# A delta-net decoder layer: beta on the scan's diagonal by ScalarE, both tables from PSUM by VectorE, the last two levels' evictions by ScalarE

## Chip, cores and metric

One core of a Trainium2 chip runs the whole program. The metric is the device time of one execution in microseconds; of several executions the median is given.

## What is computed

One pre-norm decoder layer on x of 8 x 256 tokens and 512 channels: x plus a gated delta net, plus cross attention, plus a feed-forward network. The change touches the delta net alone. Its recurrence per head, with normalised keys k, gates b (beta) and decays d, is

```
Sk    = einsum('bhi,bhipj->bhpj', k_t, state)
delta = (v_t - Sk) * b_t[..., None]
state = state * d_t + einsum('bhi,bhpj->bhipj', k_t, delta)
o     = einsum('bhi,bhipj->bhpj', q_t, state)
```

k, q and v come from a projection of the normalised x and a causal convolution with 4 taps. Behind the recurrence o is RMS-normed, multiplied by silu(z) and projected back. There are 16 key heads with 2 value heads each, and the recurrence runs over the 256 tokens of a batch element.

## The kernel before, in words

`delta_net` works in 64 sections: 16 key heads (`hk`) times 4 windows of 512 tokens (`bp`), each window two blocks of 256 tokens. A section treats NM = 4 matrices, one per block and value head. The recurrence is turned into matrix form. Two tables are made per matrix, in three 128 x 128 pieces each (TRI = 384 columns): `a_t`, keys against keys, times decay products and beta, and `b_t`, keys against queries, the same way. The decay products are a scan on VectorE (L779) over the decays, with an identity `diag` as its added operand, so that each row starts at 1 on the diagonal. The new values `delta` solve a triangular system with `a_t`: its two 128 x 128 diagonal chunks c = 0, 1 are inverted by doubling in LEVELS - 1 = 6 levels, and `b_t` then gives the output.

Each engine has its own program (`pe_section`, `act_section`, `dve_section`, the GpSimd loop), and the order of its instructions is written out by hand. Engines wait for each other by counted events, as `E["xm"]`: nothing on an engine passes a waiting instruction. While section s is inverted, the projections and convolutions of section s + 1 and the output of section s - 1 are woven into the gaps.

The order in a section:
- TensorE: transposes of v (L437), norms of the outputs of s - 1 (L445), half of the key projection (L405), start of the inverse (`pe_first`, L473). Then for each level: `pe_x` (L483, writes `xp`), half a projection of s + 1 or an output product of s - 1 (`pe_y`, L460, at levels 4 and 5), and `pe_tu` (L493, L496; L500 at level 6), which needs `x_l`, the masked copy of `xp` in SBUF. Between 5 and 6 stands one more output product. Then the solution with L506, the gate projections as fill, the products keys x keys and keys x queries of s + 1 (`pe_kq`, L425), and the output product (L576).
- VectorE: at the head of a section the a table from SBUF copies (L789, eight operations, with beta as a scalar), 1 - a (L794), the first inverse matrices (L801), gating of s - 1 (L809, L814), and per level the masked copy `x_l` (L852) and one convolution (L756, three taps). Output sums (L819) stand around levels 4 to 6. Behind the levels come the differences L827, L834, L871, the rounding L873 and the four scans.
- ScalarE: evictions of PSUM, among them `act_kq` (L714), the levels' evictions (L680), the convolution inputs (L609, L612), exponentials and logarithms, and the rounding of the right side (`v_r`, L692) at level 4.
- GpSimd: the b table from SBUF copies in 16 operations (`pool_b`, L975 to L981), the remainders of the gated outputs (L985), silu (L990), and the split of weights in two parts (L965, L967).

The eight PSUM banks are `pj0`, `pj1`, `xp0`, `xp1`, `tp`, `up`, `ms0` and `ms1`; `ms` and `up` hold the `pe_kq` products and `ms` also the norms.

Of the kernel before, what the change touches and what calls it, by code (L numbers as in the profile page):

```python
# [278 lines left out]
def delta_net(nc, y_all, xh, xl, w_d, conv_w, cols, lmask, half_mask, diag, beta, decay_rows):  # L279
# [10 lines left out]
    with ExitStack() as ctx:  # L290
        m = Memory(nc, ctx)
        NM = 2 * PV
        WC = KT * P
# [15 lines left out]
        kk = m.sb("kk_masked", [P, 2, TRI])  # L309
        qk = m.sb("qk_masked", [P, 2, TRI])  # L310
# [5 lines left out]
        kk16, ez16 = kk[:, :, :].rearrange("p b t -> p (b t)").bitcast(F16), [e[:, :].bitcast(F16) for e in ez]  # L316
        W = NM * P
        H = W // 2
        pair = [kk16[:, 0:2 * W], ez16[1][:, 0:2 * W]]
# [17 lines left out]
        tu_bank = (tp, ms[1])  # L337

        E = {}
        for name, n in dict(  # L340

                pj=4, cin=4, c3=4, cv=12, pz=2, ez=2, zc=2, e1=2, lz=2, rz=2, sz=2,
                beta_s=1, conv_t=1,

                ksq=1, kssp=1, kss=1, kln=1, krn=1, kn=1, kq=4, km=4, dec=4,

                vt=2, vc=2, vr=1, at=8, bq=8, bt0=4, bt=4, an=2, u0=2, t0=2,

                xp=2 * LEVELS - 2, xm=2 * LEVELS - 2, tu=2 * LEVELS - 2, tc=2 * LEVELS - 2, uc=2,

                d0p=2, d0=2, rd0=2, rp=2, res=2, dp2=2, delta=2, cp=1, rhs1=1, rhs1r=1,

                op=2, osq=2, oss=2, oln=2, ors=2, g1=2, g2=2, ghi=2, glo=2, y=4, yadd=4).items():
            E[name] = m.event("e_" + name, n)
# [56 lines left out]
        def pe_norms(pe, t):  # L411

            E["ksq"].wait(pe, t, 0)
            pe.matmul(ms[0][:, :], ones, ksq[:, :], start=True, stop=True).then_inc(E["kssp"].sem, 1)
# [25 lines left out]
        def pe_out_norms(pe, s, p, more):  # L440

            E["osq"].wait(pe, s, p)
            if more:
                E["km"].wait(pe, s + 1, 3)
            pe.matmul(ms[p][:, :], ones, osq[p][:, :], start=True, stop=True).then_inc(E["oss"].sem, 1)  # L445
# [19 lines left out]
        def pe_first(pe, s, c, after_out):  # L465

            E["u0"].wait(pe, s, c)
            if c == 0 and after_out:
                E["delta"].wait(pe, s + -1, 1)
            elif after_out:  # L470
                E["oln"].wait(pe, s + -1, 1)
# [15 lines left out]
        def pe_tu(pe, s, lv, c):  # L487

            E["xm"].wait(pe, s, 2 * (lv - 1) + c)
# [20 lines left out]
        def pe_section(pe, s, bp, hk, prev, nxt):  # L510
# [133 lines left out]
        def act_out_norms(act, s, p):  # L644
            E["oss"].wait(act, s, p)
            act.activation(gat[p][:, :], ms[p][:, :], ACT.Ln, scale=1.0 / P, bias=cols["rms_eps"])\
# [13 lines left out]
        def act_section(act, s, bp, hk, prev, nxt):  # L660
# [15 lines left out]
            for lv in range(1, LEVELS):  # L676
                for c in range(2):
# [27 lines left out]
            if nxt:  # L705
                act_kq(act, s + 1, 0)
                act_kq(act, s + 1, 1)
                act_kq(act, s + 1, 2)
                act_kq(act, s + 1, 3)
            act_sigmoid(act, s, 1)  # L710

        def act_kq(act, t, i):
            E["kq"].wait(act, t, i)
            act.activation((kk, qk)[i % 2][:, i // 2, :], (ms[0], ms[1], up, ms[0])[i][:, 0:TRI], ACT.Copy)\  # L714
                .then_inc(E["km"].sem, 1)

        def act_prologue(act):
            first = Section(0, 0)
            for j in range(GATE):
# [3 lines left out]
            for i in range(4):  # L723
                act_kq(act, first, i)
# [9 lines left out]
        def dve_beta(dve, s, bp, hk):  # L734

            E["bt"].wait_before(dve, s)
# [37 lines left out]
        def dve_decays(dve, t, q):  # L774

            if q == 0:
                rows_in.wait(dve, t, 31)
            i = slot(q)
            dve.tensor_tensor_scan(dec[:, i, :], dec[:, i, :], diag, 0.0, ALU.mult, ALU.add).then_inc(E["dec"].sem, 1)  # L779

        def dve_a(dve, s):

            E["km"].wait(dve, s, 3)
            E["beta_s"].wait(dve, s, 0)
            for q in range(NM):
                E["dec"].wait(dve, s, q)
                for c, sl in enumerate((slice(0, SEQ), slice(SEQ, TRI))):
                    before = dec[:, slot(q), sl.start + c:sl.stop + c]
                    dve.scalar_tensor_tensor(out=a_t[:, q, sl], in0=kk[:, q // PV, sl],  # L789
                                             scalar=beta_s[:, 2 * (q // PV) + c, q % PV:q % PV + 1], in1=before,  # L790
                                             op0=ALU.mult, op1=ALU.mult).then_inc(E["at"].sem, 1)
            E["at"].wait(dve, s, 7)
# [43 lines left out]
        def dve_section(dve, s, bp, hk, prev, nxt):  # L836
            t, nhk, nbp = s + 1, (nxt or (0, 0))[0], (nxt or (0, 0))[1]
            dve_beta(dve, s, bp, hk)
            dve_a(dve, s)
            if prev:  # L840
                dve_gated(dve, s + -1)
            if nxt:
                dve_conv_weights(dve, t, nhk)
            for lv in range(1, LEVELS):
                if lv in (5, 6) and prev:
                    dve_y(dve, s + -1, prev[1], 2 * lv - 9)
                for c in range(2):
# [5 lines left out]
                       .then_inc(E["xm"].sem, 1)  # L853
                if lv == 4 and prev:
# [19 lines left out]
            dve_gate(dve, s, 0)  # L874
            if nxt:
                dve_decays(dve, t, 1)
            dve_rest(dve, s, 1)
            if nxt:
                dve_decays(dve, t, 2)
            dve_residual(dve, s, 1)  # L880
# [3 lines left out]
            E["dp2"].wait(dve, s, 1)  # L884
            dve.tensor_tensor(delta[1], tp[:, :], d0[:, :].bitcast(F32), ALU.add).then_inc(E["delta"].sem, 1)

        def dve_prologue(dve):
# [3 lines left out]
            dve_conv_weights(dve, first, 0)  # L891
            for j in range(GATE):
# [3 lines left out]
            for q in range(NM):  # L896
                dve_decays(dve, first, q)

        def dve_epilogue(dve, s, hk):
            dve_gated(dve, s)  # L900
            for i in range(4):
# [27 lines left out]
        def load_decays(sp, hk, bp):  # L929

            if hk or bp:
                E["at"].wait(sp, hk * NSEC + bp - 1, 7)
# [36 lines left out]
        def pool_b(pool, s, q):  # L969
            E["km"].wait(pool, s, q // PV * 2 + 1)  # L970
            E["beta_s"].wait(pool, s, 0)
            if s:
                E["op"].wait(pool, s - 1, PV - 1)
            for c, sl in enumerate((slice(0, SEQ), slice(SEQ, TRI))):
                pool.tensor_scalar(b_t[:, q, sl], qk[:, q // PV, sl], beta_s[:, 2 * (q // PV) + c, q % PV:q % PV + 1],  # L975
                                   None, ALU.mult).then_inc(E["bq"].sem, 1)
            E["dec"].wait(pool, s, q)
            E["bq"].wait(pool, s, 2 * q + 1)
# [1062 lines left out]
```

## Time and profile before

| | before |
|---|---|
| median of 3 executions | 4521.77 us (4520.63 to 4523.58) |
| the profiled execution | 4521.22 us |
| its span, first to last instruction | 4519.4 us |
| TensorE matmul busy | 3998.6 us (88%) |
| VectorE busy | 3161.6 us (70%) |
| ScalarE busy | 2237.8 us (50%) |
| GpSimd busy | 1898.3 us (42%) |

The profile is one execution: 4521.22 us is its whole time, 4519.4 us the span of its instructions, and the 1.8 us between lie around them. PE is TensorE's matmuls, PEld its weight loads, DVE VectorE, ACT ScalarE, POOL GpSimd. Busy shares are of the whole span; the delta net is about its first 3100 us. In an order in time, the number in brackets is how long the engine stood idle before the row, and behind it the instruction that released it. Matmuls overlap, so the step from one start to the next is the time that one costs.

### The profile page before, as it was taken

How to read it: one execution, taken by the hardware profiler on the slowest of the kernel's cores; microseconds unless marked ns; L12 is line 12 of the kernel's file. 1: busy time of each engine (PE TensorE's matmuls, PEld its weight loads, DVE VectorE, ACT ScalarE, POOL GpSimd, SP SyncE). 2: the span in 40 equal slices, each digit the busy share in tenths (PEclk: the TensorE clock that was granted, in tenths of full speed). 3: DMA queues.
4: the chain of work that ended last, by engine and by line, in shares of the span. 5: the costliest groups of instructions: out<-in, count | busy, mean ns of one | idle time of the engine just before them, and what ended most of it. 6: DMA issues, size and time to landing. Idle time of an engine off the chain costs nothing. (4 is left out here: it accounts for less than half of the span.)

```text
span 4519.4 us, 75144 instructions
## 1 busy us (share of the span) xinstructions
PE 3998.6 (88%) x26288; PEld 2920.6 (65%) x26288; DVE 3161.6 (70%) x5082; ACT 2237.8 (50%) x4061; POOL 1898.3 (42%) x1852
## 2 busy tenths in 40 slices
PE   3899999999999999999999999995788989389998
PEld 2677777777776777767777777774344444178887
DVE  3788888888888888888888888884556556632222
ACT  1465655556565655656565565653344445221111
POOL 1365554545455554545455454543233333311110
PEclk8899999999999999999999999997799999699999
DMA  2001010101001011010101010101565563000001
GB/s 74 15 29 36 25 36 21 41 25 32 29 20 41 24 32 30 29 32 24 32 30 36 25 36 21 29 27 31 94 91 90 83 92 60 38 24 19 19 14 38
DMA packets 134066, 172.39 MB, mean 38 GB/s; under 512 B 12524, under 2 KB 79980, under 8 KB 133132
## 3 DMA queue, kind: packets, MB, share of 16 engines
q1 hardware_dynamic: 131212, 166.03, 15.9%
q8 instruction: 225, 3.69, 0.3%
q10 hardware_dynamic: 2432, 1.05, 0.2%
q14 instruction: 197, 1.61, 0.1%
HBM read 143.12 MB, written 21.76 MB: 36 GB/s over the span
## 5 line engine op out<-in xcount | busy, mean ns | idle before, releaser
L405 PE MATMUL pj<-xh,w_hi 128*128 128x512 f32 x1536 | 686.1, 447 | 26.3 <-ACT conv_k L612 17.8
L990 POOL TENSOR_TENSOR silu_z<-silu_z,exp_z 128x512 f32<-128x512 f32 x128 | 184.6, 1442 | 1216.9 <-ACT exp_z L629 1216.9
L405 PE MATMUL pj<-xh,w_lo 128*128 128x512 f32 x1536 | 608.0, 396 | 0.0
L405 PE MATMUL pj<-xl,w_hi 128*128 128x512 f32 x1536 | 603.3, 393 | 0.0
L1518 DVE TENSOR_REDUCE row_max<-s 128x1 f32<-128x512 f32 x512 | 341.9, 686 | 271.8 <-PE s L1272 268.6
L975 POOL TENSOR_SCALAR b_t<-qk_masked,beta_section 128x256 f32<-128x256 f32 (+1 forms) x512 | 490.5, 968 | 21.5 <-ACT qk_masked L714 20.2
L1452 ACT ACTIVATE probs<-s 128x512 f32<-128x512 f32 x512 | 291.3, 595 | 325.0 <-PE s L1296 319.4
L756 DVE SCALAR_TENSOR_TENSOR conv_v<-conv_in,conv_w_section,conv_v 128x512 f32<-128x512 f32 x384 | 403.7, 1051 | 20.2 <-ACT conv_v L612 9.1
L680 ACT ACTIVATE kk_masked<-tp 128x512 f16<-128x512 f32 x320 | 191.5, 598 | 323.7 <-PE tp L496 320.2
L405 PEld LDWEIGHTS pj<-xh,w_hi 128*128 128x128 f32 x1536 | 291.8, 190 | 83.3 <-issue 31.2
L405 PEld LDWEIGHTS pj<-xh,w_lo 128*128 128x128 f32 x1536 | 289.6, 189 | 67.4
L405 PEld LDWEIGHTS pj<-xl,w_hi 128*128 128x128 f32 x1536 | 293.2, 191 | 48.4 <-issue 11.7
L1296 PE MATMUL s<-q_stack,k_stack 128*128 128x512 f32 x512 | 248.9, 488 | 74.7 <-DMA q_stack<-row_maxima 66.7
L609 ACT ACTIVATE conv_in<-pj 128x512 f32<-128x512 f32 x256 | 153.7, 600 | 284.5 <-DVE conv_w_section L743 147.3
L852 DVE TENSOR_TENSOR x_l<-xp,half_mask 128x256 f16<-128x256 f32 x768 | 286.1, 412 | 9.5 <-PE xp L483 9.1
L789 DVE SCALAR_TENSOR_TENSOR a_t<-kk_masked,beta_section,decays 128x256 f32<-128x256 f32 (+1 forms) x512 | 252.0, 561 | 30.4 <-ACT qk_masked L714 28.8
L819 DVE TENSOR_TENSOR x_all<-x_all,pj 128x512 f32<-128x512 f32 x256 | 174.0, 680 | 103.5 <-PE pj L460 103.0
L779 DVE TENSOR_TENSOR_SCAN decays<-decays,scan_diag 128x386 f32<-128x386 f32 x256 | 243.8, 953 | 0.0
L1272 PE MATMUL s<-k_stack,q_stack 126*128 126x512 f32 x512 | 229.6, 451 | 15.4 <-DMA k_stack<-mask_stack 9.6
L460 PE MATMUL pj<-wo_hi,u_final 128*128 128x512 f32 x512 | 225.5, 440 | 19.8 <-issue 14.2
L979 POOL TENSOR_TENSOR b_t<-b_t,decays 128x256 f32<-128x256 f32 x256 | 216.2, 844 | 39.2 <-POOL b_t L975 1.8
L1296 PEld LDWEIGHTS s<-q_stack,k_stack 128*128 128x128 f32 x512 | 98.3, 193 | 189.2 <-ACT probs L1452 100.7
(259 smaller groups left out, 10250.9 us busy)
## 6 DMA issues: line engine op xcount, KB each, us to landing
w_raw<-in_w_in SPq DMA_DIRECT2D x128, 256.0 KB, 3.5
decays<-decay_by_head SPq DMA_DIRECT2D x64, 512.0 KB, 3.8
decays<-decay_by_head SPq DMA_DIRECT2D x64, 256.0 KB, 4.9
q_stack<-qk_parts SPq DMA_DIRECT2D x128, 128.0 KB
k_stack<-qk_parts SPq DMA_DIRECT2D x128, 128.0 KB
f_raw<-in_f_w SPq DMA_DIRECT2D x32, 256.0 KB, 2.7
x_all<-in_x SPq DMA_DIRECT2D x4, 1024.0 KB, 11.5
source<-in_ctx SPq DMA_DIRECT2D x8, 512.0 KB
```

Source lines behind the costliest of these rows:

```text
L405: mm = pe.matmul(pj[j % 2][:, :], a[:, j, k * P:(k + 1) * P], b[:, k, bp * WIN:(bp + 1) * WIN], start=(n == 0), stop=(n == 3 * KT - 1))
L460: mm = pe.matmul(pj[i % 2][:, :], a[p][:, i * P:(i + 1) * P], b[:, p, :], start=(n == 0), stop=(n == 3 * PV - 1))
L756: dve.scalar_tensor_tensor(out=out, in0=cin[j % 2][:, :, tap:tap + SEQ], scalar=conv_t[:, j * TAPS + tap:j * TAPS + tap + 1], in1=out, op0 ...
L779: dve.tensor_tensor_scan(dec[:, i, :], dec[:, i, :], diag, 0.0, ALU.mult, ALU.add).then_inc(E["dec"].sem, 1)
L789: dve.scalar_tensor_tensor(out=a_t[:, q, sl], in0=kk[:, q // PV, sl], scalar=beta_s[:, 2 * (q // PV) + c, q % PV:q % PV + 1], in1=before, ...
L852: dve.tensor_tensor(out, of, keep.to_broadcast([P, NM, P >> (lv + 1), 1 << lv]), ALU.mult)\
L975: pool.tensor_scalar(b_t[:, q, sl], qk[:, q // PV, sl], beta_s[:, 2 * (q // PV) + c, q % PV:q % PV + 1], None, ALU.mult).then_inc(E["bq"]. ...
L979: pool.tensor_tensor(b_t[:, q, 0:SEQ], b_t[:, q, 0:SEQ], dec[:, slot(q), 1:SEQ + 1], ALU.mult)\
L1272: pe.matmul(s1[n % 2][:, :], qs[f][0:R_MAX, h, tt * P:(tt + 1) * P], ks[f][0:R_MAX, h, :], start=True, stop=True).then_inc(E["s1"].sem, 1)
L1296: pe.matmul(s2[n % 2][:, :], ks[f][:, h, st * P:(st + 1) * P], qs[f][:, h, :], start=True, stop=True).then_inc(E["s2"].sem, 1)
L1452: act.activation(pt[:, n % RP, :], s2[n % 2][:, :], ACT.Exp).then_inc(E["ex"].sem, 1)
L1518: dve.reduce_max(mx[g % 2][:, i:i + 1], s1[n % 2][:, :], AX_X).then_inc(E["rm"].sem, 1)
```

## The change

Beta leaves the table operations and goes into the scan: ScalarE writes beta times the identity into `beta_diag`, eight operations of 128 columns (`act_beta`), and the scan adds that in place of the identity. Each table is then one product of decays and PSUM, made by VectorE in four operations for both value heads at once (`dve_table`); `act_kq`, `pool_b` and the SBUF copies `kk`, `qk` go. The a table is made at the end of the section before. The remainders of the gated outputs move from GpSimd to VectorE, behind level 2. At levels 5 and 6 ScalarE evicts `xp` to `x_l`, only the rows and columns of the odd blocks, in two operations per tile at level 5 and one at level 6. The `pe_kq` products are made in another order (both key products first), the first norm of the outputs goes to bank `tp`, and `pe_section` places the key products ahead of the second solution.

```diff
         def pe_kq(pe, t, i):
             if i == 0:
                 E["kn"].wait(pe, t, 0)
+            if i == 2:
                 E["cv"].wait(pe, t, QUERY * 3 + 2)
             if i == 3:
-                E["km"].wait(pe, t, 0)
-            bank = (ms[0], ms[1], up, ms[0])[i]
-            right, o = (kn, cv[QUERY])[i % 2], (i // 2) * SEQ
+                E["at"].wait(pe, t, 1)
+            bank, right, o = kq_bank[i], (kn, cv[QUERY])[i // 2], (i % 2) * SEQ
...
             pe_group(pe, up, lambda q: a_t[:, q, P:SEQ], delta[0], "cp")
-            proj(GATE + 1, 0)
-            E["rhs1r"].wait(pe, s, 0)
             E["uc"].wait(pe, s, 1)
-            pe_group(pe, xp[0], lambda q: u_f[:, 1, mat(q)], v_r, "d0p")
-            proj(GATE + 1, 1)
-            E["d0"].wait(pe, s, 1)
-            pe_group(pe, xp[1], lambda q: a_t[:, q, SEQ:TRI], d0[:, :].bitcast(F32), "rp")
             if nxt:
                 pe_kq(pe, s + 1, 0)
                 pe_kq(pe, s + 1, 1)
+            E["rhs1r"].wait(pe, s, 0)
+            pe_group(pe, xp[0], lambda q: u_f[:, 1, mat(q)], v_r, "d0p")
+            proj(GATE + 1, 0)
+            E["d0"].wait(pe, s, 1)
+            pe_group(pe, xp[1], lambda q: a_t[:, q, SEQ:TRI], d0[:, :].bitcast(F32), "rp")
+            proj(GATE + 1, 1)
...
             for lv in range(1, LEVELS):
+                if lv >= WIDE:
+                    for c in range(2):
+                        act_x(act, s, lv, c)
                 for c in range(2):
                     E["tu"].wait(act, s, 2 * (lv - 1) + c)
...
                     act.activation(v_r[:, :], v_t[:, 0, :], ACT.Copy).then_inc(E["vr"].sem, 1)
+                    if nxt:
+                        act_beta(act, s + 1)
                 if lv == 5 and nxt:
                     act_square(act, s + 1, s)
...
+        def act_x(act, s, lv, c):
+            E["xp"].wait(act, s, 2 * (lv - 1) + c)
+            b = 1 << lv
+            for n in range(P // (2 * b)):
+                rows = slice(2 * b * n + b, 2 * b * (n + 1))
+                act.activation(by_mat(x_l[c][lv - 1][rows, :])[:, :, 2 * b * n:2 * b * n + b],
+                               xp[c][rows, 0:H].rearrange("p (m n i) -> p m n i", m=NM, i=b)[:, :, n, :], ACT.Copy)\
+                   .then_inc(E["xa"].sem, 1)
+
+        def act_beta(act, t):
+            E["beta_s"].wait(act, t, 0)
+            E["dec"].wait_before(act, t)
+            for q in range(NM):
+                for c in range(2):
+                    o = c * (SEQ + 1) + 1
+                    act.activation(beta_diag[:, slot(q), o:o + P], ident, ACT.Copy,
+                                   scale=beta_s[:, 2 * (q // PV) + c, q % PV:q % PV + 1]).then_inc(E["bd"].sem, 1)
...
-            dve.tensor_tensor_scan(dec[:, i, :], dec[:, i, :], diag, 0.0, ALU.mult, ALU.add).then_inc(E["dec"].sem, 1)
+            dve.tensor_tensor_scan(dec[:, i, :], dec[:, i, :], beta_diag[:, i, :], 0.0, ALU.mult, ALU.add).then_inc(E["dec"].sem, 1)
+
+        def dve_table(dve, t, b, c, out, kq, done, after):
+            E["kq"].wait(dve, t, kq)
+            E["dec"].wait(dve, t, b * PV + PV - 1)
+            sl = (slice(0, SEQ), slice(SEQ, TRI))[c]
+            o = c + after
+            dve.tensor_tensor(out[:, b * PV:(b + 1) * PV, sl], dec[:, b:NM:2, sl.start + o:sl.stop + o],
+                              kq_bank[kq][:, sl].unsqueeze(1).to_broadcast([P, PV, sl.stop - sl.start]), ALU.mult)\
+               .then_inc(E[done].sem, 1)
...
-            dve_beta(dve, s, bp, hk)
-            dve_a(dve, s)
+            dve_inverse(dve, s)
+            dve_b(dve, s, prev)
             if prev:
                 dve_gated(dve, s + -1)
             if nxt:
                 dve_conv_weights(dve, t, nhk)
+                dve_beta(dve, t, nbp, nhk)
             for lv in range(1, LEVELS):
                 if lv in (5, 6) and prev:
                     dve_y(dve, s + -1, prev[1], 2 * lv - 9)
-                for c in range(2):
+                for c in range(2 if lv < WIDE else 0):
...
+                if lv == 2 and prev:
+                    for p in range(PV):
+                        dve_gated_rest(dve, s + -1, p)
...
-                    for q in range(NM):
-                        pool_b(pool, s, q)
-                    if s:
-                        for p in range(PV):
-                            pool_gated_rest(pool, s - 1, p)
```

`WIDE` is 5. In the order lists below the names are the program's tiles: `t_and_u` is the new buffer for the first tile's inverse, which before lay in `kk_masked`; line numbers are those of each program.

ScalarE, from level 4 of a section to its last eviction, before:

```order
L680 ACTIVATE kk_masked<-tp 128x2x16x16
L680 ACTIVATE exp_z<-ms 128x2x16x16
L692 ACTIVATE rhs_rounded<-v_tok 128x512
L680 ACTIVATE kk_masked<-tp 128x2x8x32
L680 ACTIVATE exp_z<-ms 128x2x8x32
L635 ACTIVATE square<-conv_k 128x512
L684 ACTIVATE u_final<-tp 128x512
```

and now:

```order
L687 ACTIVATE t_and_u<-tp 128x2x16x16
L687 ACTIVATE exp_z<-ms 128x2x16x16
L699 ACTIVATE rhs_rounded<-v_tok 128x512
L733 ACTIVATE beta_diag<-consts,beta_section 128x128 x8
L722 ACTIVATE x_l_5<-xp 32x4x32 x4
L687 ACTIVATE t_and_u<-tp 128x2x8x32
L687 ACTIVATE exp_z<-ms 128x2x8x32
L639 ACTIVATE square<-conv_k 128x512
L722 ACTIVATE x_l_6<-xp 64x4x64 x2
L691 ACTIVATE u_final<-tp 128x512
```

Eight products for the next section and four evictions stand between the rounding and level 5's eviction, and two more ahead of the last.

VectorE, from the rounding of the second right side to the head of the next section, before:

```order
L873 CAST rhs_rounded<-v_tok 128x512
L764 TENSOR_SCALAR exp_z<-exp_z 128x512
L779 SCALAR_TENSOR_TENSOR decays<-decays,scan_diag 128x386
L827 TENSOR_TENSOR v_tok<-v_tok,delta_first 128x512
L779 SCALAR_TENSOR_TENSOR decays<-decays,scan_diag 128x386
L834 TENSOR_TENSOR residual<-v_tok,xp 128x512
L764 TENSOR_SCALAR exp_z<-exp_z 128x512
L779 SCALAR_TENSOR_TENSOR decays<-decays,scan_diag 128x386
L885 TENSOR_TENSOR v_tok<-tp,delta_first 128x512
L737 TENSOR_SCALAR beta_section<-beta 128x8
L789 SCALAR_TENSOR_TENSOR a_t<-kk_masked,beta_section,decays 128x256
L789 SCALAR_TENSOR_TENSOR a_t<-kk_masked,beta_section,decays 128x128
```

and now:

```order
L913 CAST rhs_rounded<-v_tok 128x512
L799 SCALAR_TENSOR_TENSOR decays<-decays,beta_diag 128x386
L783 TENSOR_SCALAR exp_z<-exp_z 128x512
L863 TENSOR_TENSOR v_tok<-v_tok,delta_first 128x512
L807 TENSOR_TENSOR a_t<-decays,ms 128x2x256
L870 TENSOR_TENSOR residual<-v_tok,xp 128x512
L807 TENSOR_TENSOR a_t<-decays,ms 128x2x128
L799 SCALAR_TENSOR_TENSOR decays<-decays,beta_diag 128x386
L925 TENSOR_TENSOR v_tok<-tp,delta_first 128x512
L783 TENSOR_SCALAR exp_z<-exp_z 128x512
L799 SCALAR_TENSOR_TENSOR decays<-decays,beta_diag 128x386
L807 TENSOR_TENSOR a_t<-decays,ms 128x2x256
```

The a table's pieces stand among the scans, two of them ahead of the last delta (L925); eight operations from SBUF copies behind it are gone.

VectorE, from the last gating product to level 3, before:

```order
L814 TENSOR_TENSOR square<-square,silu_z 128x512
L743 TENSOR_SCALAR conv_w_section<-conv_w 128x16
L852 TENSOR_TENSOR x_l_1<-xp,half_mask 128x128x2 x2
L756 SCALAR_TENSOR_TENSOR conv_k<-conv_in,conv_w_section,conv_k 128x512 x3
L852 TENSOR_TENSOR x_l_2<-xp,half_mask 128x64x4 x2
L756 SCALAR_TENSOR_TENSOR conv_q<-conv_in,conv_w_section,conv_q 128x512 x3
L852 TENSOR_TENSOR x_l_3<-xp,half_mask 128x32x8 x2
```

and now:

```order
L850 TENSOR_TENSOR square<-square,silu_z 128x512
L762 TENSOR_SCALAR conv_w_section<-conv_w 128x16
L756 TENSOR_SCALAR beta_section<-beta 128x8
L889 TENSOR_TENSOR x_l_1<-xp,half_mask 128x128x2 x2
L775 SCALAR_TENSOR_TENSOR conv_k<-conv_in,conv_w_section,conv_k 128x512 x3
L889 TENSOR_TENSOR x_l_2<-xp,half_mask 128x64x4 x2
L823 TENSOR_TENSOR delta_first<-rnorm,u_final 128x512
L823 TENSOR_TENSOR residual<-square,u_final 128x512
L775 SCALAR_TENSOR_TENSOR conv_q<-conv_in,conv_w_section,conv_q 128x512 x3
L889 TENSOR_TENSOR x_l_3<-xp,half_mask 128x32x8 x2
```

Beta stands ahead of level 1, and the two remainders behind level 2. The four pieces of the b table stand earlier, between the first inverse matrices and the gating.

## Rows read from the trace of the kernel before

**Rows 1.** Transposes of v, line L437: durations ns, first and last start, forms.
```profile
L437 PE MATMUL pj<-consts,conv_v x512: 272/273/328, 137.6 to 3058.8; 128*128 128x128 f32 x171
```

**Rows 2.** Busy us of PE, PEld, DVE, ACT, POOL; granted clock, DMA share, GB/s.
```profile
1000.00:1500.00 500.00, 467.66 (x3506) 357.08 (x3506) 421.49 (x668) 298.99 (x543) 263.83 (x263) 1.00 0.10 29
```

**Rows 3.** Waits, TensorE weight loads, 183 to 2925 us: total us, times, longest.
```profile
PEld tp L493 <- DVE x_l L852: 166.9, 291, 1.9
```

**Rows 4.** Order in time, TensorE, one section: start, us, operation [idle before <-releaser].
```profile
1485.91 0.40 PE L473 MATMUL tp<-ident,kk_masked 128*128 128x128 f16 x4 [0.31 <-DVE kk_masked L801]
...
1489.41 0.40 PE L405 MATMUL pj<-xh,w_lo 128*128 128x512 f32 x1
1489.84 0.29 PE L493 MATMUL tp<-x_l,kk_masked 128*128 128x64 f16 x4
...
1493.93 0.30 PE L493 MATMUL tp<-x_l,kk_masked 128*128 128x64 f16 x4 [0.16 <-DVE x_l L852]
...
1500.38 0.49 PE L460 MATMUL pj<-wo_hi,u_final 128*128 128x512 f32 x1 [0.33 <-POOL residual L985]
...
1505.10 0.39 PE L460 MATMUL pj<-wo_lo,u_final 128*128 128x512 f32 x1
1505.34 0.40 PE L460 MATMUL pj<-wo_hi,residual 128*128 128x512 f32 x1
1505.99 0.29 PE L493 MATMUL tp<-x_l,kk_masked 128*128 128x64 f16 x4 [0.26 <-DVE x_l L852]
...
1508.05 0.29 PE L483 MATMUL xp<-kk_masked,i_minus_a 128*128 128x64 f16 x4
1508.18 0.28 PE L483 MATMUL xp<-exp_z,i_minus_a 128*128 128x64 f16 x4
1509.32 0.40 PE L500 MATMUL tp<-kk_masked,x_l 128*128 128x128 f16 x4 [0.86 <-DVE x_l L852]
...
1518.28 0.67 PE L506 MATMUL xp<-rhs_rounded,u_final 128*128 128x128 f32 x4
```

**Rows 5.** VectorE groups by shape, 183 to 2925 us: busy us, mean ns | idle.
```profile
L852 DVE TENSOR_TENSOR x_l<-xp,half_mask 128x256 f16<-128x256 f32 x708 | 263.3, 411 | 0.0
...
L834 DVE TENSOR_TENSOR residual<-v_tok,xp 128x512 fp32r<-128x512 f32 x118 | 80.7, 684 | 14.1 <-PE xp L506 14.1
...
L737 DVE TENSOR_SCALAR beta_section<-beta 128x8 f32 x56 | 35.1, 627 | 30.1 <-issue 30.1
```

**Rows 6.** Order in time, ScalarE, the section of rows 4.
```profile
1485.35 0.63 ACT L649 ACTIVATE square<-square 128x512 f32<-128x512 f32 x1
...
1493.14 0.63 ACT L658 ACTIVATE u_final<-rnorm 128x512 fp32r<-128x512 f32 x1
1493.67 0.63 ACT L658 ACTIVATE u_final<-square 128x512 fp32r<-128x512 f32 x1
...
1503.30 0.63 ACT L692 ACTIVATE rhs_rounded<-v_tok 128x512 fp32r<-128x512 f32 x1
```

**Rows 7.** Order in time, VectorE, the section of rows 4.
```profile
1489.08 0.38 DVE L743 TENSOR_SCALAR conv_w_section<-conv_w 128x16 f32 x1
...
1497.62 3.77 DVE L756 SCALAR_TENSOR_TENSOR conv_v<-conv_in,conv_w_section,conv_v 128x512 f32<-128x512 f32 x3 [0.16 <-ACT conv_v L612]
...
1502.68 2.32 DVE L756 SCALAR_TENSOR_TENSOR conv_v<-conv_in,conv_w_section,conv_v 128x512 f32<-128x512 f32 x3
...
1517.80 0.43 DVE L873 CAST rhs_rounded<-v_tok 128x512 fp32r<-128x512 f32 x1
```

**Rows 8.** ScalarE groups by shape, 183 to 2925 us: busy us, mean ns | idle.
```profile
L680 ACT ACTIVATE kk_masked<-tp 128x512 f16<-128x512 f32 x295 | 176.5, 598 | 291.9 <-PE tp L496 288.4
...
L714 ACT ACTIVATE qk_masked<-ms 128x384 f32<-128x384 f32 x118 | 57.4, 487 | 9.7 <-PE ms L427 9.7
...
L692 ACT ACTIVATE rhs_rounded<-v_tok 128x512 fp32r<-128x512 f32 x59 | 37.4, 634 | 0.0
...
L612 ACT ACTIVATE conv_k<-pj,conv_w_section 128x512 f32<-128x512 f32 x59 | 40.2, 682 | 0.0
```

More of the change, by code:

```diff
@@ L292, in delta_net @@
         NM = 2 * PV
+        WIDE = 5
         WC = KT * P
@@ L443, in pe_out_norms @@
             if more:
-                E["km"].wait(pe, s + 1, 3)
-            pe.matmul(ms[p][:, :], ones, osq[p][:, :], start=True, stop=True).then_inc(E["oss"].sem, 1)
+                E["at"].wait(pe, s + 1, 3)
+            pe.matmul(sum_bank[p][:, :], ones, osq[p][:, :], start=True, stop=True).then_inc(E["oss"].sem, 1)
         def pe_y(pe, s, hk, i, bank_read):
@@ L467, in pe_first @@
             E["u0"].wait(pe, s, c)
[L468 to L471, printed above, removed]
+            if after_out:
+                E["oln"].wait(pe, s + -1, c)
             for q in range(NM):
@@ L487, in pe_tu @@
         def pe_tu(pe, s, lv, c):
-            E["xm"].wait(pe, s, 2 * (lv - 1) + c)
+            if lv < WIDE:
+                E["xm"].wait(pe, s, 2 * (lv - 1) + c)
+            else:
+                E["xa"].wait(pe, s, 2 * c + 1 if lv == WIDE else 4 + c)
             x = x_l[c][lv - 1]
@@ L777, in dve_decays, with dve_a, dve_b, dve_gated_rest @@
                 rows_in.wait(dve, t, 31)
+                E["bd"].wait(dve, t, 7)
             i = slot(q)
-            dve.tensor_tensor_scan(dec[:, i, :], dec[:, i, :], diag, 0.0, ALU.mult, ALU.add).then_inc(E["dec"].sem, 1)
-        def dve_a(dve, s):
-            E["km"].wait(dve, s, 3)
-            E["beta_s"].wait(dve, s, 0)
-            for q in range(NM):
[L786 to L792, printed above, removed]
+            dve.tensor_tensor_scan(dec[:, i, :], dec[:, i, :], beta_diag[:, i, :], 0.0, ALU.mult, ALU.add).then_inc(E["dec"].sem, 1)
[7 more added lines that the diff above has]
+               .then_inc(E[done].sem, 1)
+        def dve_a(dve, t, b, c):
+            dve_table(dve, t, b, c, a_t, b, "at", 0)
+        def dve_b(dve, s, prev):
+            if prev:
+                E["op"].wait(dve, s + -1, PV - 1)
+            for b in range(2):
+                for c in range(2):
+                    dve_table(dve, s, b, c, b_t, 2 + b, "bt", 1)
+        def dve_gated_rest(dve, s, p):
+            E["ghi"].wait(dve, s, p)
+            dve.tensor_tensor(g_lo[p][:, :], gat[p][:, :], g_hi[p][:, :].bitcast(F32), ALU.subtract)\
+                .then_inc(E["glo"].sem, 1)
+        def dve_inverse(dve, s):
+            E["at"].wait(dve, s, 3)
             for c, sl in enumerate((slice(0, P), slice(SEQ, TRI))):
@@ L873, in dve_section @@
             dve.tensor_copy(v_r[:, :], v_t[:, 1, :]).then_inc(E["rhs1r"].sem, 1)
-            dve_gate(dve, s, 0)
             if nxt:
                 dve_decays(dve, t, 1)
+            dve_gate(dve, s, 0)
             dve_rest(dve, s, 1)
             if nxt:
+                dve_a(dve, t, 0, 0)
+            dve_residual(dve, s, 1)
+            if nxt:
+                dve_a(dve, t, 0, 1)
                 dve_decays(dve, t, 2)
-            dve_residual(dve, s, 1)
+            E["dp2"].wait(dve, s, 1)
+            dve.tensor_tensor(delta[1], tp[:, :], d0[:, :].bitcast(F32), ALU.add).then_inc(E["delta"].sem, 1)
             dve_gate(dve, s, 1)
@@ L883, in dve_section @@
                 dve_decays(dve, t, 3)
-            E["dp2"].wait(dve, s, 1)
-            dve.tensor_tensor(delta[1], tp[:, :], d0[:, :].bitcast(F32), ALU.add).then_inc(E["delta"].sem, 1)
+                dve_a(dve, t, 1, 0)
+                dve_a(dve, t, 1, 1)
         def dve_prologue(dve):
@@ L891, in dve_prologue @@
             dve_conv_weights(dve, first, 0)
+            dve_beta(dve, first, 0, 0)
             for j in range(GATE):
@@ L897, in dve_prologue @@
                 dve_decays(dve, first, q)
+            for b in range(2):
+                for c in range(2):
+                    dve_a(dve, first, b, c)
         def dve_epilogue(dve, s, hk):
             dve_gated(dve, s)
+            for p in range(PV):
+                dve_gated_rest(dve, s, p)
             for i in range(4):
@@ L997, in _ @@
             pool.memset(dec[:, :, SEQ + 1:SEQ + 2], 0.0).then_inc(pads, 1)
+            pool.memset(beta_diag[:, :, :], 0.0).then_inc(pads, 1)
             split_weights(pool, 0, range(PIECES))
@@ L1016, in _ @@
                         pool_silu(pool, s, p)
-            for p in range(PV):
-                pool_gated_rest(pool, HK * NSEC - 1, p)
         @block.scalar
```

69 lines of the change are left out of this document (20 added, 49 removed).

## Prediction

> **What bounds the kernel now.** I read the spread over time first, then the averages of the stage that the change touches, then who waits for whom, and last the order in time of one section on three engines. The delta net takes 64 sections. The transposes of v stand at the head of each, and the first and last of them start 2921 us apart [rows 1], 46.4 us a section. In a piece of it TensorE is busy 94% of the time, VectorE 84%, ScalarE 60% and GpSimd 53%, at a granted clock of 1.00, the upper level of 2.4 GHz [rows 2]. So TensorE is the bound, and no matmul is added or removed: only the time in which it stands still can be won. Most of that goes to VectorE: its weight loader waited 166.9 us for the masked eviction x_l alone [rows 3].
>
> The waits of one section, begun at 1481.45, are in [rows 4]. The reader should add to each bracket the overlap that a wait also destroys: products start 0.23 to 0.24 us apart though each lasts 0.40, and groups of four small matmuls 0.13 apart though each lasts 0.29, so 0.16 to 0.17 goes on top. That gives: start of the inverse (L473) 0.31 + 0.17 = **0.48**; level 1, where no idle time is shown but the step is 0.43 instead of 0.23, with the second tile's smaller wait **0.28**; level 2, 0.16 + 0.17, with the second tile **0.40**; the output product (L460), which waits for GpSimd's remainder, 0.33 + 0.16 = **0.49**; level 5, 0.26 + 0.17, with the second tile **0.50**; level 6, 0.86 + 0.16 = **1.02**. Sum 3.17 us of some 46.
>
> **The change, part by part**, in that same section.
>
> *Tables.* Before, ScalarE copies four products to SBUF, VectorE makes the a table in eight operations and GpSimd the b table in sixteen. Now VectorE makes each in four, from PSUM. No row shows a product with an operand repeated out of PSUM. The bounds are 0.41 us for 256 elements, as x_l takes with a PSUM operand, and 0.68 for 512, as the residual does [rows 5]; I take these, since the elements are as many, and successive starts 0.08 less. One table is then 1.9 us, both 3.8. The a table now ends before the section does, so the inverse can start about 1 us ahead of the section's head and the first matrices are there 2.7 us before TensorE wants them: the 0.48 goes. What is late next is only ScalarE's logarithm of the norms, which frees the bank just in time. b follows and ends 1.3 us before the second rsqrt (1485.35 + 0.63 = 1485.98 [rows 6]), which the gating needs anyway: it is hidden by that much.
>
> *Level 1.* From 1485.98 VectorE has one gating product of 0.65, two of 0.60, the convolution weights 0.30 (0.38 long [rows 7]) and now also beta 0.55 (0.63 long [rows 5]), then x_l 0.41: the operand stands at 1489.14. TensorE, 0.48 earlier, wants it at 1489.16. With the second tile I leave **0.10** of the 0.28. Level 2's 0.40 goes, because the first convolution starts sooner and has no GpSimd beside it.
>
> *Remainders.* Both now go on VectorE behind level 2, where they wait for ScalarE's roundings; the second ends at 1493.67 + 0.63 [rows 6], 0.66 earlier in the new frame. Remainders to 1494.4, the q convolution 2.3 to 1496.7, x_l 0.41 to 1497.1. TensorE, by now 1.06 ahead of the old times, would want level 3 at 1496.6: **a new wait of 0.53** with both tiles. In exchange the 0.49 at the output product goes. The 2.3 is the row of three convolution steps with an idle GpSimd, against 3.77 for the same three with GpSimd busy [rows 7]: that is what taking the work off GpSimd brings to VectorE.
>
> *Beta on the diagonal and the wide evictions.* This is where the change costs. Eight 128-column multiplications are put on ScalarE between rounding the right side (1503.30 [rows 6]) and the two evictions of level 5. From 512 to 384 columns a copy falls from 0.598 to 0.487, so 128 columns are 0.111; an SBUF source costs 0.04 more, a scale from memory 0.08 more [rows 8]. That makes 0.598 - 0.333 + 0.12 = 0.38 each. Two roundings from SBUF that last 0.63 start 0.53 apart [rows 6], so I take 0.28 as their step and 2.24 us for eight. The ends are 0.15 (the narrowest step worked out the same way from 384 columns, 0.37 - 0.22) and 0.38 (no overlap); 0.28 is taken since its rows are back-to-back SBUF operations of this engine. TensorE is now 1.02 ahead. ScalarE comes to level 5 at 1503.30 - 1.02 + 0.53 + 2.24 = 1505.05; two evictions of a 32-partition block (0.27 each, 0.18 apart) free the first tile at 1505.55 with 0.05 of signalling. TensorE would want it at 1505.34 + 0.23 - 1.02 = 1504.55. So the wait is 1.0, with the second tile **1.10**, where it was 0.50. At level 6 ScalarE has nothing ahead: 0.29 for the group, 0.04, a 256-column eviction of 0.38, 0.04 put the next step 0.75 after L483 instead of 1.27, so **0.50** of the 1.02 stays.
>
> *The order on TensorE.* Two table products now stand where half a projection stood, ahead of the product with the rounded right side (1518.28 [rows 4]). They take 1.30 us instead of 1.48, and VectorE's rounding ends at 1517.80 + 0.43 [rows 7], which just fitted: **0.20** is lost. Behind it, half a projection now covers the residual, the old order having nothing there; delta is ready 0.4 us before the output product wants it, though a table piece and a scan now stand in front of it. The four ScalarE copies that go (1.9 us) and the beta products that come (2.2) nearly cancel in its queue. The decays' transfer is issued sooner and lands earlier; it was never waited for. The memset of the diagonal runs on GpSimd while it waits for its first weights: nothing.
>
> *Sum.* New waits 0.20 + 0.10 + 0.53 + 1.10 + 0.50 = 2.43 against 3.17, a gain of 0.74 us a section. Times the 62 sections that have both neighbours: 46 us. Once, ahead of the first convolution, eight beta products add 2.3 us. The profiled execution takes 4521.2 us, 0.6 below the median of the runs: 4521.2 - 46 + 2.3 = **4478 us**. In the sections where GpSimd splits weights the old waits are longer; I count no more for them, as the splits also move onto other convolutions.
>
> **The rivals.**
> - *Cheap small operations* (0.18). If a beta product takes a step of 0.17, ScalarE reaches level 5 0.88 sooner and the gain is 1.62 a section: 4521 - 100 + 2 = 4423. For it: the subtraction from 384 columns. Against: the rows with a memory scale.
> - *ScalarE becomes the bound at level 5* (0.17), the side on which it gets slower. If the small operations do not overlap, eight cost 3.04 (0.80 more) and the evictions 0.25 more: 1.05 against a gain of 0.74, 0.31 lost a section, 4521 + 19 + 2 = 4542. It decides from a step of 0.37 per beta product. Against it: the overlap of 0.10 [rows 6]. The Trainium skill, page "VectorE: DVE Perf Modes", section on the TRN2 errata, has a rule that speaks for this rival: the latency of SBUF is exposed between instructions, so many small tiles pay it each time, and it advises tiles of at least 512 elements. By that rule the result would be the 4542 of this rival; the overlapping rows here speak against it.
> - *VectorE becomes the bound at level 1* (0.07). If the repeated PSUM operand halved the rate, the six table pieces ahead of the gating would take about 3 us more than 2.85; 1.3 of it is covered, the rest delays x_l by some 1.7: 1.0 lost a section, 4585. It decides from 2.0 us more. The residual's 0.68 with PSUM speaks against it.
> - *The waits only move* (0.08): the level 3 wait doubles to 1.2, because the remainders wait for roundings behind a busier ScalarE, and the gain is below 0.15 a section: within 9 us of before.
>
> **How the numbers follow.** My forecast, 4450 to 4505, has 0.50. A measurement of this kernel can tell 0.2%, 9 us, from no change. Faster by more than that: 0.50 + 0.18 = 0.68. Within: 0.08. Slower: 0.17 + 0.07 = 0.24. The range 4418 to 4550 takes in the cheap case and ScalarE as the bound, and leaves out VectorE as the bound and the lower end of the cheap step.
>
> **What would show it.** Right: no wait at L473's successor and at the output product; the largest new wait at level 5, 1.0 us, released by ScalarE's eviction; level 6 down to half; beta products 0.38 long and 0.28 apart; convolution steps near 0.78 in sections without splits; section period near 45.7. Wrong: a wait at level 1 above 0.5 released by x_l, table pieces above 0.75, or a level 5 wait below 0.3.

## The result, and the profile after

The changed kernel takes 4551.84 us (median of 4, 4547.09 to 4554.25) against 4521.20 us before: a ratio of 1.0066, 95% interval 1.0049 to 1.0084. It is 0.7% slower, where I forecast 1% faster, and just outside my range. The profiled execution has a span of 4551.6 us. Its page, busy time by engine:

```profile
PE 3983.9 (88%) x26288; PEld 2939.2 (65%) x26288; DVE 3005.9 (66%) x4954; ACT 2376.8 (52%) x4701; POOL 816.4 (18%) x701
```

VectorE lost 156 us of busy time, GpSimd 1082, ScalarE gained 139. So the change did move the work that it says, and TensorE still has the same 26288 matmuls. The transposes of v at the section heads, and the waits of TensorE's matmuls from 183 to 2925 us (total us, times, longest):

```profile
L440 PE MATMUL pj<-consts,conv_v x512: 272/273/328, 137.2 to 3094.6; 128*128 128x128 f32 x171
```

```profile
PE tp L497 <- ACT x_l L722: 68.2, 58, 1.2
PE tp L497 <- DVE x_l L889: 67.9, 58, 3.9
PE tp L504 <- ACT x_l L722: 20.6, 58, 0.4
PE ms L497 <- ACT x_l L722: 10.4, 58, 0.2
```

From first to last start it is 2957.4 us where it was 2921.2 [rows 1]: 36 us more, against 32 for the whole span, so all of the loss is in the delta net. The waits for ScalarE's evictions come 58 times, once a section, and the longest is 1.2 us, near their mean. The wait for VectorE's x_l also comes 58 times, but its longest is 3.9 us and its mean 1.2: it isn't the same in every section. That is the line to follow. I took the start of every section from the order in time of the whole stage and sorted the sections by their place in the head. Mean length in us, and the step from the matmul before to the first of the level:

| section of a head | first | second | third | fourth |
|---|---|---|---|---|
| length before | 47.39 | 45.34 | 46.42 | 46.28 |
| length after | 47.61 | 44.82 | 49.56 | 45.83 |
| step to level 3, before | 1.06 | 0.23 | 0.24 | 0.24 |
| step to level 3, after | 0.69 | 0.69 | 3.86 | 0.69 |
| step to level 5, before | 0.71 | 0.64 | 1.31 | 0.54 |
| step to level 5, after | 1.57 | 1.57 | 1.57 | 1.57 |

Second and fourth sections did get shorter, by 0.5 us. The first got 0.2 us longer and the third 3.1, and 16 third ones outweigh the rest. The last head has no next head whose weights GpSimd would split, and its third section took 44.83 us, as a second one does; the 15 others took 49.2 to 50.9. One third section, begun at 1543.94, on TensorE:

```profile
1558.67 0.40 PE L407 MATMUL pj<-xh,w_lo 128*128 128x512 f32 x1
1562.61 0.40 PE L497 MATMUL tp<-x_l,t_and_u 128*128 128x64 f16 x4 [3.55 <-DVE x_l L889]
...
1563.46 0.78 PE L407 MATMUL pj<-xh,w_hi 128*128 128x512 f32 x1
1564.04 0.63 PE L407 MATMUL pj<-xl,w_hi 128*128 128x512 f32 x1
1564.46 0.63 PE L407 MATMUL pj<-xh,w_lo 128*128 128x512 f32 x1
```

TensorE stands still for 3.55 us in front of level 3. What VectorE and GpSimd do meanwhile:

```profile
1555.44 1.37 DVE L823 TENSOR_TENSOR delta_first<-rnorm,u_final 128x512 fp32r<-128x512 f32 x1 [0.35 <-ACT u_final L662]
1556.74 1.09 DVE L823 TENSOR_TENSOR residual<-square,u_final 128x512 fp32r<-128x512 f32 x1
1557.76 4.47 DVE L775 SCALAR_TENSOR_TENSOR conv_q<-conv_in,conv_w_section,conv_q 128x512 f32<-128x512 f32 x3
1562.15 0.74 DVE L889 TENSOR_TENSOR x_l<-xp,half_mask 128x256 f16<-128x256 f32 x2
```

```profile
1554.15 0.74 POOL L1016 CAST w_hi<-w_raw 128x512 fp32r<-128x512 f32 x1 [9.04 <-DMA w_raw<-in_w_in]
1554.98 1.29 POOL L1018 TENSOR_TENSOR w_lo<-w_raw,w_hi 128x512 fp32r<-128x512 f32 x1
1556.21 1.07 POOL L1016 CAST w_hi<-w_raw 128x512 fp32r<-128x512 f32 x1
1557.37 1.62 POOL L1018 TENSOR_TENSOR w_lo<-w_raw,w_hi 128x512 fp32r<-128x512 f32 x1
1558.94 1.07 POOL L1016 CAST w_hi<-w_raw 128x512 fp32r<-128x512 f32 x1
1560.09 1.58 POOL L1018 TENSOR_TENSOR w_lo<-w_raw,w_hi 128x512 fp32r<-128x512 f32 x1
```

The three steps of the q convolution take 4.47 us instead of 2.32, and the remainders 1.37 and 1.09 instead of 0.69: GpSimd splits three pieces of the next head's weights beside them. Before, that split began 21.9 us into the third section begun at 1526.79; now it begins 10.2 us in:

```profile
1548.70 0.61 POOL L965 CAST w_hi<-w_raw 128x512 fp32r<-128x512 f32 x1 [3.29 <-DMA w_raw<-in_w_in]
```

And the wait has a price on top. Busy us of PE, PEld, DVE, ACT and POOL, granted clock, DMA share and GB/s, in the end of the stretch of waiting and behind it:

```profile
1558.00:1562.60 4.60, 1.07 (x5) 0.54 (x3) 4.53 (x5) 0.72 (x2) 3.59 (x3) 0.94 0.27 88
1562.60:1565.30 2.70, 2.69 (x20) 2.32 (x21) 2.45 (x4) 1.08 (x2) 0.00 (x0) 0.50 0.00 0
```

For 2.7 us behind the standstill the granted clock is 0.50, the lower level of 1.2 GHz, and the products start 0.43 apart instead of 0.23. From the first product of level 3 to L484 (1562.61 to 1565.85) it is 3.24 us, where the same products at level 2, without a wait, take 1.95: about 1.2 us more than in a second section, which has a small wait of 0.09 there. The step to level 3 is 3.94 here against 0.69 in second sections, 3.25 more. Both together are about 4.5, and this section, 49.24 us long, is 4.4 longer than a second one.

### The profile page after: what moved, and what is told of

The parts are those of the page before. It is cut to its first block and busy times, and to the rows that moved or that the text cites. A ratio compares the mean times of both kernels' runs of the same rounds, so it can differ in the third digit from the quotient of the medians.

```text
span 4551.6 us, 75144 instructions
## 1 busy us (share of the span) xinstructions
PE 3983.9 (88%) x26288; PEld 2939.2 (65%) x26288; DVE 3005.9 (66%) x4954; ACT 2376.8 (52%) x4701; POOL 816.4 (18%) x701
## 3 DMA queue, kind: packets, MB, share of 16 engines
q1 hardware_dynamic: 131068, 165.84, 15.7%
## 5 line engine op out<-in xcount | busy, mean ns | idle before, releaser
L775 DVE SCALAR_TENSOR_TENSOR conv_v<-conv_in,conv_w_section,conv_v 128x512 f32<-128x512 f32 x384 | 287.6, 749 | 11.6 <-ACT conv_v L616 2.5
L687 ACT ACTIVATE t_and_u<-tp 128x512 f16<-128x512 f32 x320 | 191.1, 597 | 179.3 <-PE tp L500 177.4
L799 DVE TENSOR_TENSOR_SCAN decays<-decays,beta_diag 128x386 f32<-128x386 f32 x256 | 243.6, 952 | 0.0
L624 ACT ACTIVATE exp_z<-pj 128x512 f32<-128x512 f32 x128 | 76.4, 597 | 309.4 <-PE pj L407 309.4
L497 PE MATMUL tp<-x_l,t_and_u 128*128 128x64 f16 x1280 | 94.8, 197 | 146.8 <-ACT x_l L722 76.0
L497 PEld LDWEIGHTS tp<-x_l,t_and_u 128*128 128x128 f16 x1280 | 56.3, 99 | 253.3 <-DVE x_l L889 131.4
L863 DVE TENSOR_TENSOR v_tok<-v_tok,delta_first 128x512 f32<-128x512 f32 x128 | 98.8, 772 | 168.0 <-ACT delta_first L705 154.4
```

The lines of the kernel that those rows point to most:

```text
L687: act.activation(half_pair(c, lv), tu_bank[c][:, :].rearrange("p (a n i) -> p a n i", a=2, i=1 << lv), ACT.Copy)\
L775: dve.scalar_tensor_tensor(out=out, in0=cin[j % 2][:, :, tap:tap + SEQ], scalar=conv_t[:, j * TAPS + tap:j * TAPS + tap + 1], in1=out, op0 ...
L799: dve.tensor_tensor_scan(dec[:, i, :], dec[:, i, :], beta_diag[:, i, :], 0.0, ALU.mult, ALU.add).then_inc(E["dec"].sem, 1)
```

## The experiments

Two causes stood against each other: the collision of the split with VectorE in third sections, and the beta products in front of level 5, which I had as the rival on the slower side. All runs of a group share their executions of the kernel before, whose median was 4520 to 4524 us in the three groups; ratios are to that, with 95% intervals.

**split_late.** One wait for GpSimd.

```diff
                     if hk < HK - 1 and bp == 2:
+                        E["cv"].wait(pool, s + 1, (VALUE + PV - 1) * 3 + 2)
                         split_weights(pool, hk + 1, range(GATE))
```

> The changed kernel with one wait added on GpSimd: in every third section of a head the split of the next head's weights starts only when VectorE has finished the last convolution (the second v). Collision theory: the changed kernel is slow because that split, now freed of the b table ahead of it, runs beside the remainders and the q convolution on VectorE. Then the step to level 3 in third sections falls from 3.9 us to the 0.7 of the other sections, the granted clock stays at 1.00 there, the third sections fall from 49.6 to about 46 us, and the time is 4552 - 15 x 3.5 = about 4500 us (4490 to 4510). Theory of the beta products (ScalarE is the bound at level 5 in every section): the time stays within 10 us of 4552.

Measured 4480.87 us, ratio 0.9915 (0.9899 to 0.9932). In the order in time of a third section, begun at 1512.26, on VectorE and GpSimd:

```profile
1524.95 2.32 DVE L775 SCALAR_TENSOR_TENSOR conv_q<-conv_in,conv_w_section,conv_q 128x512 f32<-128x512 f32 x3
```

```profile
1534.63 0.61 POOL L1016 CAST w_hi<-w_raw 128x512 fp32r<-128x512 f32 x1 [21.20 <-DVE conv_v L775]
```

The q convolution is back at 2.32, the step to level 3 of third sections is 0.70, and their length 45.43. The other sections did not move (47.61, 44.83, 45.85). One wait more made the kernel 71 us faster, 10 us below the range of the expectation: that counted 3.5 us for each of the 15 sections, but they fell by 4.4 on average, 66 us together, as 1.2 us for the clock go with 3.2 of waiting. The load of the weights is still issued 5.3 us into the section, and the first two of its four transfers land 10.1 and 10.7 us in, as in the changed kernel (10.2 and 11.0), so it isn't those transfers that stretch the convolution. Nor is the late split free: third sections stay 0.6 above second ones, as it now stretches VectorE's difference L863 (1.81 us instead of 0.69) and TensorE waits at the solution's products.

**sp_hold.** GpSimd's program stays as changed; SyncE holds the load of the weights.

```diff
                 if hk < HK - 1:
+                    E["cv"].wait(sp, hk * NSEC + 3, VALUE * 3 + 2)
                     load_weights(sp, hk + 1, range(4))
```

> The changed kernel, with GpSimd's program untouched: only SyncE holds back the load of the next head's weights until VectorE has finished the first v convolution, so that the split of them begins about where it began before the change, 19 to 22 us into the third section. Collision theory: it is the moment of the split that costs, so the level 3 step of third sections falls from 3.9 to 0.7 us and the time to within 15 us of split_late (4481). If the cost came from GpSimd's or VectorE's own order, it stays near 4552.

Measured 4480.78 us, ratio 0.9912 (0.9895 to 0.9928), third sections 45.14. The first conversion of the split, in the third section begun at 1511.14, shows who holds it now:

```profile
1531.93 0.61 POOL L1017 CAST w_hi<-w_raw 128x512 fp32r<-128x512 f32 x1 [19.61 <-DMA w_raw<-in_w_in]
```

So only the moment matters, and SyncE's queue sets it. There the weights' load stands behind the decays' load, which waits for the last piece of the b table (`load_decays`). Before, GpSimd finished that table at 1542.5 in the third section begun at 1526.79, 15.7 us in. VectorE now does so at 1548.18 in the one begun at 1543.94, 4.2 us in. SyncE issues the load right behind it, 16.7 us in before (first row) and 5.3 now (second):

```profile
1543.50 10.24 SPq L927 DMA_DIRECT2D w_raw<-in_w_in  x4
```

```profile
1549.21 10.13 SPq L978 DMA_DIRECT2D w_raw<-in_w_in  x4
```

**before_late.** The same line as in split_late, in the kernel before.

> The kernel before the change, with the late split alone. There the split already began 22 us into the third section, beside the last convolution, and level 5 waited 0.7 us longer than in the other sections. Collision theory: about 15 x 0.7 = 10 us less than 4521, and no more. If third sections were slow for another reason, nothing changes.

Measured 4503.99 us, ratio 0.9956 (0.9939 to 0.9972). Third sections fall from 46.42 to 45.55 and their step to level 5 from 1.31 to 0.54. First sections fall by 0.2. The collision was there before, with the last convolution, and cost some 20 us, twice what I put on it and more than the "no more" of the expectation. So with the split late in both kernels the change is worth 4504 to 4481, 23 us (19 by the two ratios, as the runs are of different groups).

**beta_spread.** The beta products in two groups of four, out of level 5's way.

```diff
+                if lv == 3 and nxt:
+                    act_beta(act, s + 1, (0, 1))
                 if lv == 4:
                     E["vc"].wait(act, s, 0)
                     act.activation(v_r[:, :], v_t[:, 0, :], ACT.Copy).then_inc(E["vr"].sem, 1)
-                    if nxt:
-                        act_beta(act, s + 1)
...
             if nxt:
+                act_beta(act, s + 1, (2, 3))
                 act_norms(act, s + 1)
```

> The changed kernel with the eight beta products taken out from ahead of level 5's evictions: four behind the third level's convolution input, four behind the first eviction of d0, both in idle time of ScalarE. Theory of the beta products: the step to level 5 falls from 1.57 us to below 0.6 in every section and the time falls by some 62 x 1.2 = 75 us to about 4475. Collision theory: the same level 5 gain, but third sections still stand about 3.7 us above second ones, with a level 3 step of about 3.9 us.

Measured 4443.46 us, ratio 0.9831 (0.9814 to 0.9847): 108 us less than the changed kernel. The step to level 5 is 0.24 in every section, no wait at all, and the second tile's went from 0.46 to 0.12; with it the gain is 1.67 a section, of which the expectation had 1.2, and so 75 us. Third sections are still 4.9 us longer than second ones. Its waits:

```profile
PE tp L497 <- DVE x_l L890: 68.1, 60, 4.0
PE tp L504 <- ACT x_l L723: 21.3, 60, 0.4
```

The line of L497 waiting for ScalarE is gone, that for VectorE unchanged. Both costs are real; how far they are independent, the next run shows.

**both.** 

> Both edits together. If the two costs are independent, the gains add: about 4552 - 52 - 75 = 4425 us (4410 to 4445), below the kernel before at 4521. If one only moves into the other's wait, it stays above 4460.

Measured 4380.59 us, ratio 0.9687 (0.9671 to 0.9703). 71 and 108 add up to 179, and 171 came: the two costs are independent but for 8 us. It is 29 us below the expected range, as each of the two gains was larger than expected.

**dve_wide.** `WIDE = LEVELS` in the changed kernel: VectorE evicts all levels.

> The changed kernel with levels 5 and 6 evicted by VectorE again, as before; the beta products stay where they are. Theory of the beta products: the step to level 5 falls from 1.57 to about 0.6 us, the step to level 6 rises from 0.63 to 1.15 us, net about 0.5 us less a section and 4552 - 30 = 4522 us. If the evictions by ScalarE are worth their place even behind the beta products, the time rises by up to 30 us.

Measured 4501.94 us, ratio 0.9958 (0.9944 to 0.9972). Behind the beta products, ScalarE's evictions cost 50 us more than VectorE's, where I expected 30: the step to level 5 falls from 1.57 to 0.66 and its second tile's by another 0.25, that to level 6, taken from the start of the group before it, rises from 0.63 to 1.15. Second sections are 0.65 shorter (44.17 against 44.82). The edit that was to spare TensorE a wait made one, for its place in the queue.

**best_dve_wide.** The same edit in the last kernel below.

> rest_l3_gate (4337 us) with levels 5 and 6 evicted by VectorE again. With the beta products out of the way, ScalarE's evictions should be worth what I forecast for them: level 5 then waits 0.4 us behind VectorE's output sum and level 6 0.5 us more than with ScalarE, so 62 x 1.0 = about 60 us more, 4395 (4375 to 4410). If VectorE, now free of GpSimd, reaches them in time, the time stays within 15 us of 4337.

Measured 4381.10 us, ratio 0.9692 (0.9676 to 0.9708): 44 us more than with ScalarE. With the queue free the sign turns round. Both parts came as expected: the step to level 5 rises from 0.24 to 0.66 and that to level 6 from 0.63 to 1.15, and second sections are 1.0 longer (43.58 against 42.57). Third and first sections are only 0.5 and 0.4 longer, so it is 44 us and not 60. The waits:

```profile
PE tp L504 <- DVE x_l L890: 51.2, 59, 0.9
PE tp L497 <- DVE x_l L890: 17.0, 59, 0.4
```

**rest_l3.** In `both`, the remainders moved behind level 3.

```diff
-                if lv == 2 and prev:
+                if lv == 3 and prev:
                     for p in range(PV):
                         dve_gated_rest(dve, s + -1, p)
```

> The kernel with both edits (late split, spread beta products), and the two remainders moved from behind level 2 to behind level 3 on VectorE. If they are what delays the q convolution and with it the level 3 copy, the step to level 3 falls from 0.70 to 0.24 us in every section, no new wait shows at the output product or level 4, and the time falls by 62 x 0.5 = 31 us from 4381 to about 4350. If VectorE's queue is full there, the wait shows again at level 4 and the time stays within 10 us.

Measured 4345.71 us, ratio 0.9616 (0.9600 to 0.9632). The step to level 3 is 0.24 in all sections, nothing shows at level 4.

**rest_pool.** In `both`, the remainders back on GpSimd.

> The kernel with both edits, and the two remainders put back on the now idle GpSimd. They run beside the k and q convolutions there. If the contention between the two engines is what counts, the q convolution is longer than 2.32 us and level 3 keeps a wait of 0.3 us or more (4370 to 4395); if only VectorE's number of operations counts, the step to level 3 falls to 0.24 us and the time to about 4350.

Measured 4401.41 us, ratio 0.9738 (0.9721 to 0.9754), 21 us more than `both`, 56 more than rest_l3 and 6 above the expected range, though VectorE has two operations less. The step to level 3 is 0.92 in second sections. VectorE's q convolution, by shape (busy us, mean ns), first here and then in rest_l3:

```profile
L776 DVE SCALAR_TENSOR_TENSOR conv_q<-conv_in,conv_w_section,conv_q 128x512 f32<-128x512 f32 x177 | 240.3, 1358 | 4.1
```

```profile
L776 DVE SCALAR_TENSOR_TENSOR conv_q<-conv_in,conv_w_section,conv_q 128x512 f32<-128x512 f32 x180 | 134.8, 749 | 4.2
```

1358 ns against 749 for the same operation. Two subtractions on GpSimd, 3 us of its time, stretch the convolution by 1.8 us. The mean is 1357 to 1360 ns in all four kinds of section, also in those in which no weights are split or loaded, so the subtractions alone do this. It's the contention that counts, not the number of operations.

**rest_l3_gate.** rest_l3, and the split of the gate weights in first sections waits for the last convolution too.

> As rest_l3, and in first sections GpSimd's split of the gate weights also waits for the last convolution. Collision theory: it now runs beside 1 - a and the gating (x1 step 0.79 us in first sections against 0.23 in the others), so 15 x 0.6 us = 9 us less than rest_l3. Otherwise within 4 us of it.

Measured **4337.12 us**, ratio 0.9591 (0.9575 to 0.9607), the fastest of all: 4.1% below the kernel before. First sections fall from 45.43 to 44.67 us and their step before level 1 from 0.89 to 0.30. The waits that are left:

```profile
PE xp L510 <- ACT u_final L691: 26.1, 60, 0.5
PE tp L504 <- ACT x_l L723: 21.3, 60, 0.4
```

Both are the short chain at level 6, and no wait for x_l from VectorE is among the largest any more. First sections are still 2.1 us above second ones, in waits at their head and at the solution's products that no run here takes apart.

## Why the prediction was wrong

The forecast was 4478 us, the result 4552. The walk through a second section held, in most of its terms; the forecast failed on sections that it left out.

1. *Start of the inverse, 0.48 gone*: right. The step is 0.24 in second, third and fourth sections. Table pieces take 0.68 and 0.41, as the rows that I took said.
2. *Level 1, 0.10 left*: nothing is left, and nothing at level 2. The weights and beta take 0.16 us each instead of the 0.38 and 0.63 of before.
3. *Level 3, a new wait of 0.53*: right, 0.46 for the first tile and 0.09 for the second.
4. *Level 5, 1.10*: too small, it is 1.34 + 0.34 = 1.68. The eight beta products are as forecast, but the four narrow evictions start 0.29 apart and not 0.18, which is about 0.36 of the 0.58 that I missed. The other 0.22 is that TensorE gets there 22.88 us into the section and not 23.10. ScalarE, in the second section begun at 1499.10:

```profile
1520.24 2.44 ACT L733 ACTIVATE beta_diag<-consts,beta_section 128x128 f32<-128x128 f32 x8
1522.71 1.15 ACT L722 ACTIVATE x_l<-xp 32x128 f16<-32x128 f32 x4
```

   With a duration of 0.40, eight in 2.44 us are a step of 0.29. By shape, duration of one (mean ns):

```profile
L733 ACT ACTIVATE beta_diag<-consts,beta_section 128x128 f32<-128x128 f32 x464 | 141.6, 397 | 0.0
L722 ACT ACTIVATE x_l<-xp 32x128 f16<-32x128 f32 x232 | 62.3, 268 | 5.7
```

   Four evictions in 1.15 at 0.27 each are the same 0.29. My 0.18 came from subtracting columns from a wide copy; the step doesn't fall that far.
5. *Level 6, 0.50 left*: right, 0.51.
6. *Order on TensorE, 0.20*: nothing there. The product with the rounded right side starts 0.21 behind the table products, which follow each other at 0.22.
7. *Eight beta products ahead of the first convolution, 2.3*: nothing. The first transposes start at 137.2, as before.
8. *Sum, 0.74 us a section*: second sections gained 0.52, fourth 0.45. For 62 sections that would be 31 us, 4490 us, inside the range. The items above leave 0 + 0 + 0.54 + 1.68 + 0.51 = 2.73 of waits against 3.17, a gain of 0.44; the rest of the 0.52 I did not follow.

The step that failed is the one behind the sum: "In the sections where GpSimd splits weights the old waits are longer; I count no more for them, as the splits also move onto other convolutions." The rows had all of it. The price was in [rows 7], 3.77 against 2.32, and I used it as a gain only. The Trainium skill says it in a line, too (page "GPSIMD Engine Reference", section "Key points"): GpSimd shares its SBUF interfaces with VectorE and contends with operations that have two SBUF inputs; the convolution's step of 1.36 against 0.75 us agrees. The same goes for "The decays' transfer is issued sooner and lands earlier; it was never waited for": I didn't ask what stands behind it in SyncE's queue. That is the weights' load, and with it the split. split_late and sp_hold show that the early split costs 71 us. That is close to the 74 between forecast and result, but not the same sum: some 20 of the 71 were in the kernel before as well (before_late), and so in what I started from. By the lengths of the sections, the 74 are made up like this: third sections, 3.14 longer instead of 0.74 shorter, give 62 us; first ones, 0.23 longer instead of 0.74 shorter, give 15, and GpSimd splits the gate weights there, which the same step of the prediction left out (with that split late, rest_l3_gate took 0.8 off each); second and fourth ones give 8; the very first section (2.1 shorter), the 2.3 that never came and the rest of the program take about 11 back.

My rival on the slower side, ScalarE as the bound at level 5 by full-length operations, came near the measured time with 4542, but that is luck: it rests on a step of 0.38 for each beta product, and the beta products do overlap, by 0.10, as [rows 6] had it. Of the rule of the Trainium skill that I cited there (page "VectorE: DVE Perf Modes", section on the TRN2 errata), that many small tiles pay a latency each time, a part is borne out: a step is 0.29 us for 128 columns and 0.52 for the 512 of the rounding ahead of them, so a quarter of the columns takes more than half the time. What isn't borne out is that nothing of it overlaps, 0.40 long at a step of 0.29. Still, beta_spread shows that this block was the larger of the two costs, 108 us. I had its wait in my sum at two thirds of its size.

## What to carry to other kernels

When an edit frees an engine early, list what is queued behind the wait that it releases, on SyncE too, and see what that work will run beside. Walk through one section of each kind, not only through the commonest. And small jobs for a "half idle" engine have to go where nobody waits behind them: the same beta products cost 108 us in one place and no wait that the profile shows in another.

## What the runs showed of the hardware

- GpSimd's elementwise operations on SBUF stretch VectorE's with two SBUF inputs: the q convolution 1358 against 749 ns a step, and in the third section 1.49 us. The copies with a PSUM operand do not change: in the kernel before, x_l copies beside a GpSimd operation took 0.409 us on average and those beside none 0.414 (0.411 over all [rows 5]).
- Very short VectorE operations (the convolution weights, 128x16, and beta, 128x8) took 0.35 and 0.63 us on average before, nearly all beside a busy GpSimd, and 0.16 now with GpSimd idle. The few whose address is fixed took 0.38 and 0.60 before and 0.16 now, so an address from a register isn't what makes them long; what does, no run takes apart.
- ScalarE operations of 128 columns start 0.29 us apart, whether from SBUF with a scale from memory (0.40 long) or from PSUM (0.27 long).
- After 3.55 us without work TensorE had a granted clock of 0.50 for the next 2.7 us; the waits of 1.2 us at level 5 show no such drop, the mean over the stage in split_late being 1.00.
